# A Fourier neural operator's mixing weights centred on GpSimd instead of VectorE

## The chip, the cores and the metric

One core of one Trainium2 chip runs the whole program. The metric is the device time of one execution in microseconds (us). The engines are TensorE (PE), VectorE (DVE), ScalarE (ACT), GpSimd (POOL) and SyncE (SP), which issues all transfers.

## What is computed

The input is 64 images of 64 x 64 pixels. A Fourier neural operator comes first, then a small transformer-like tower on the resulting 64 x 64 tokens per image. Cut to the part that matters:

```python
h = layer_norm(x @ fc0_w + fc0_b, ln0_g, ln0_b)
for i in range(LAYERS):                      # 4 layers, 32 channels
    x_ft = rfft2(h)
    out_ft[:, :, :M1, :M2] = einsum('bixy,ioxy->boxy', x_ft[:, :, :M1, :M2], w1)
    out_ft[:, :, -M1:, :M2] = einsum('bixy,ioxy->boxy', x_ft[:, :, -M1:, :M2], w2)
    h = irfft2(out_ft) + einsum('bchw,oc->bohw', h, conv_w[i]) + conv_b[i]
    h = layer_norm(h, ln_g[i], ln_b[i])      # over the channels
    if i < LAYERS - 1:
        h = gelu(h)
h = fc3(gelu(fc2(gelu(fc1(h)))))
...
```

w1 and w2 are complex, 32 x 32 channels times 12 x 12 modes each, and differ by layer.

## The kernel before

**Phases.** The program has five phases over the pixels with a mixing between each two: "first" (fc0, layer norm, forward transform), mixing of layer 0, "mid" three times (inverse transform, convolution, layer norm, gelu, forward transform), each followed by a mixing, and "last" with the pointwise network. The token part follows. A phase handles 16 groups of four images. The groups run in hardware loops: two groups written out, two loops of six groups, one loop of two, and the end written out.

**The order.** Each engine goes through a group by the table `ORDER`: a list of steps per engine and phase. A name is a step, the number behind the point is which of its parts, a minus sign behind it says that it belongs to the group before. The steps of PE are `xt` (input transposed) or `i1` (first half of the inverse transform, L1181), `acc` (second half, the convolution added, L1209 and L1217; in first the product with fc0, L1199), `turn` (normalised values transposed, L1235), `back` (transposed again, L1246), `f1` and `f2` (forward transform, L1260, L1274). ScalarE copies PSUM out (`acc`, L1371), squares (`sq`, L1381), applies gain, bias and gelu (`gelu`, L1392), copies rows (`back`, L1396) and stores the spectrum (`pack`, L1402). VectorE transposes 32 x 32 blocks out of PSUM (`i1`, L1512; `f1`, L1544; `f2`, L1550), sums squares (`red`, L1519), takes the inverse root by seven small instructions (`rs`, function `root`, L209 to L215) and scales (`scale`, L1533). `i1`, `f1` and `f2` share one PSUM bank pair, pD; `acc` uses pA alone, `turn` pT alone.

**The centring.** Layer norm subtracts the channels' mean, so the kernel takes it out of the weights instead: from every mixing weight the mean over the 32 output channels is subtracted. The weights of a layer lie in `w_sb` as two slots of 128 partitions x 32 x 144 values (slot 0 also has its sign turned on half of the partitions). Step `cen` of VectorE does it by slices of 24 modes: `cen.0` reduces over the channels (L1494), `cen.1` scales the sum to minus the mean (L1496), `cen.2` adds it to the weights (L1498). `inline` sets the slice by the loop's counter: six slices of slot 0 in the first loop of six groups and six of slot 1 in the second, 36 instructions per layer, whose number the semaphore `w_centred` counts. Outside these two loops `cen` is skipped. The mixing on PE waits for all 36 (L1140 are its matmuls). SyncE issues the weight loads (L972) in the phase ahead of the mixing: at its beginning in first, behind the first group's `y_in` loads in mid. GpSimd has nothing to do up to the last mixing; then it clears some memory and later splits the token part's weights into two halves of precision (L824, L826).

Of the kernel before, what the change touches and what calls it, by code (L numbers as in the profile page):

```python
# [51 lines left out]
def constants():  # L52
# [45 lines left out]
    for b in range(2):  # L98
        for q in range(M1 + 1):
            iy[:, b, q, b] = np.cos(ang(q, y))  # L100
        for q in range(1, M1 + 1):
# [41 lines left out]
    "w_loaded":      (0, 8 * 16, 0, 0),  # L143
    "w_centred":     (0, 36, 0, 0),
    "y_bias":        (0, 1, 0, 0),
# [6 lines left out]
    "first": {  # L152
        "PE": ("xt.0 turn.2- acc.0 back.2- turn.3- acc.1 back.3- acc.2 turn.0 f1.1- acc.3 f1.0- back.0 turn.1 f2.0- "
               "back.1 f2.1-"),
        "ACT": ("xt.0 gelu.2- acc.0 sq.0 back.2- gelu.3- acc.1 sq.1 back.3- acc.2 sq.2 gelu.0 acc.3 sq.3 back.0 "
                "gelu.1 back.1 pack.0- pack.1-"),
        "DVE": ("red.0 cen.0 rs.0 scale.0 red.1 rs.1 f1.1- scale.1 f1.0- red.2 red.3 f2.0- rs.2 f2.1- scale.2 rs.3 "
                "cen.1 scale.3 cen.2"),
    },
    "mid": {  # L160
        "PE": ("i1.0 turn.2- back.1- acc.0 i1.1 turn.3- back.2- acc.1 back.3- acc.2 f1.1- turn.0 f1.0- acc.3 f2.0- "
               "turn.1 f2.1- back.0"),
        "ACT": ("back.1- acc.0 sq.0 gelu.3- back.2- acc.1 sq.1 back.3- acc.2 sq.2 gelu.0 acc.3 sq.3 pack.0- gelu.1 "
                "back.0 pack.1- gelu.2"),
        "DVE": ("red.3- i1.0 rs.3- scale.3- cen.0 cen.1 i1.1 red.0 rs.0 scale.0 red.1 rs.1 f1.1- scale.1 red.2 f1.0- "
                "rs.2 f2.0- cen.2 scale.2 f2.1-"),
    },
# [50 lines left out]
def build(nc, ins, out_ap, B):  # L218
# [18 lines left out]
    with ctx:  # L237
# [48 lines left out]
        cbias, cb_sum, cv_sum = small[:, 352:384], small[:, 384:385], small[:, 388:392]  # L286
        w_mean = small[:, 400:424]

# [22 lines left out]
        def param(rows, cols):  # L311
# [48 lines left out]
                 "turned", "h_new_ok", "x_loaded", "y_loaded", "y_clear", "packed", "h_loaded0", "h_loaded1", "stored0", "stored1", "fc0_clear", "y_stored", "w_loaded",  # L360
                 "w_centred", "mix_a_full", "mix_a_free", "mix_b_full", "mix_b_free", "y_bias", "conv_cleared", "conv_loaded", "conv_chain", "cst_loaded", "ln_loaded",
                 "fc0_loaded", "fc0_chain", "mlp_cleared", "mlp_loaded", "normed", "eps_set"]
# [467 lines left out]
        def alone(eng):  # L830

            eng.sem_inc(s["passed"], 1)
# [269 lines left out]
        @block.gpsimd  # L1102
        def _(pool):
            L = LAYERS - 1
            pool.wait_ge(s["mix_a_full"], at("mix_a", "mix", L, 0, 12))
            pool.wait_ge(s["mix_b_full"], at("mix_b", "mix", L, 0, 12))
            pool.memset(w_sb[:, 0:1024], 0.0).then_inc(s["mlp_cleared"], 1)
            pool.wait_ge(s["mlp_cleared"], 1)
            pool.memset(spec[:, 0:at_col[0]], 0.0).then_inc(s["par_cleared"], 1)
            pool.wait_ge(s["par_cleared"], 1)  # L1110

            pool.memset(XT[64:128, :], 0.0).then_inc(s["ones_set"], 1)
            pool.wait_ge(s["ones_set"], 1)
            pool.memset(XT[64:65, :], 1.0).then_inc(s["ones_set"], 1)
            pool.wait_ge(s["ones_set"], 2)
            token_pool(pool)
# [3 lines left out]
        def _(pe):  # L1120
            pe.wait_ge(s["cst_loaded"], 16)

            def mix(L):
                pe.wait_ge(s["w_centred"], at("w_centred", "mix", L, 0, 36) + 1)
                alone(pe)
# [312 lines left out]
        def _(dve):  # L1438
            dve.memset(pD[:], 0.0).then_inc(s["d_free"], 1)
            dve.sem_inc(s["a_free"], 1)  # L1440
            dve.sem_inc(s["w_centred"], 1)
            for i in range(2):
# [15 lines left out]
            def mix(L):  # L1458
# [10 lines left out]
                for k in range(12):  # L1469
# [4 lines left out]
                    if k == 1:  # L1474
# [5 lines left out]
                                                 in1=dc, op0=ALU.mult, op1=ALU.add).then_inc(s["y_bias"], 1)  # L1480

            centring = {}

            def cen(n, g):

                L, i, part = centring["L"], centring["i"], centring["part"]
                w = w_v[:, part, :, bass.ds(24 * i, 24)]
                first = 18 * part + n
                if n == 0 and part == 0:
                    dve.wait_ge(s["w_loaded"], 128 * L + 128)  # L1490
                dve.wait_ge(s["w_centred"], at("w_centred", "mix", L, 0, first) + 1 + 3 * i)
                alone(dve)
                if n == 0:
                    ins_ = dve.reduce_sum(w_mean, w.rearrange("p o m -> p m o"), axis=AX)  # L1494
                elif n == 1:
                    ins_ = dve.tensor_scalar(w_mean, w_mean, const["sign"][:, 1:2] if part == 0 else -1.0 / C, None, ALU.mult)  # L1496
                else:
                    ins_ = dve.scalar_tensor_tensor(out=w, in0=w, scalar=const["sign"][:, 0:1] if part == 0 else 1.0,  # L1498
                                                    in1=w_mean.rearrange("p (o m) -> p o m", o=1).broadcast_to([P, C, 24]),
                                                    op0=ALU.mult, op1=ALU.add)  # L1500
                ins_.then_inc(s["w_centred"], 1)

            def steps(p):
# [48 lines left out]

                return dict(cen=cen, i1=i1, red=red, rs=rs, scale=scale, turn=turn, f1=f1, f2=f2)

# [5 lines left out]

            phases(dve, "DVE", mix, steps, before_last, centring)
            token_dve(dve)
# [30 lines left out]
```

## Time and profile before

| | |
|---|---|
| runs | 3419.32, 3420.4, 3575.1 us; median 3420.4 us |
| profiled execution, own time | 3420.23 us |
| span of its profile | 3418.5 us |
| instructions profiled | 77905 |
| mean granted clock of TensorE | 0.936 of full |

The span is the time from the first instruction that the profile shows to the end of the last. Below, "busy" is the time in which an engine executes, "idle before" the time the engine stood still ahead of an instruction, and the name behind "<-" what it waited for. L numbers are lines of the kernel. The sections of the page are: busy times by engine, the span in 40 slices, transfers, the chain that ended last, groups of instructions, and the transfers' issues.

### The profile page before, as it was taken

Reading aid. Unit: us, or ns where it says so; the run is one execution under the profiler, and the core shown is the slowest. Engines: PE = TensorE matmul, PEld = TensorE weight load, DVE = VectorE, ACT = ScalarE, POOL = GpSimd, SP = SyncE. Lnnn points to the kernel's source line nnn. Section 1 sums busy time; section 2 is a strip of 40 time slices with the busy share of each in tenths; the row PEclk is TensorE's granted clock in tenths of the full one; section 3 lists DMA queues with packets and bytes.
Section 4 is the critical chain, followed back from the end, with each engine's and each line's share of the span. In section 5 each row is a group of like instructions: output and inputs, shape, how many; then the busy total and the mean of one; then the engine's idle time right before and its main releaser. Section 6 shows DMA issues by size and latency. Waiting matters only on the chain.

```text
span 3418.5 us, 77905 instructions
## 1 busy us (share of the span) xinstructions
PE 2958.7 (87%) x29936; PEld 1877.1 (55%) x29936; DVE 2143.1 (63%) x3982; ACT 1960.9 (57%) x2300; POOL 28.0 (1%) x12
## 2 busy tenths in 40 slices
PE   6888859999859999859999859999999997983994
PEld 3445446666546666536666534444444446971894
DVE  5888738888638888638888724454444535236457
ACT  5777626666526666526666517777777762432451
POOL 0000000000000000000000010000000001000000
PEclk9999879999979999969999979999999997996897
DMA  4222364444464444464444444111111100000000
GB/s 118 93 96 93 109 163 159 165 165 161 150 156 159 158 168 163 144 151 172 158 158 165 137 106 92 46 56 53 56 44 44 53 1 1 1 1 0 1 1 13
DMA packets 114136, 335.43 MB, mean 98 GB/s; under 512 B 46040, under 2 KB 78040, under 8 KB 78168
## 3 DMA queue, kind: packets, MB, share of 16 engines
q1 hardware_dynamic: 114008, 333.50, 30.4%
q8 instruction: 107, 1.75, 0.2%
q14 instruction: 21, 0.17, 0.0%
HBM read 179.31 MB, written 154.14 MB: 98 GB/s over the span
## 4 chain that ended last, share of the span: by engine, by line
PE 72%; DVE 13%; issue 5%; ACT 4%; DMA 3%; SPq 1%; DVEq 0%; ACTq 0%
PE pA L1209 14%; PE pA L1217 7%; PE pT L1303 7%; PE pD L1260 4%; PE pT L1235 4%; PE pD L1292 4%; PE pD L1274 4%; PE pD L467 3%; PE pA L467 3%; PE pS L1246 3%; PE pD L1181 3%; DVE arena L1550 2%; DVE w_sb L1533 2%; DVE arena L1544 2%; PE pT L459 2%
## 5 line engine op out<-in xcount | busy, mean ns | idle before, releaser
L1519 DVE TENSOR_REDUCE small<-w_sb 128x32 f32<-128x1056 f32 x320 | 395.5, 1240 | 341.6 <-ACT w_sb L1381 339.0
L1209 PEld LDWEIGHTS pA<-conv_bd,h_in 128*128 128x128 f32 x4096 | 482.2, 193 | 121.4 <-issue 96.7
L1209 PE MATMUL pA<-conv_bd,h_in 128*128 128x128 f32 x4096 | 521.3, 281 | 15.3 <-ACT w_sb L1371 4.3
L1371 ACT COPY w_sb<-pA 128x1024 f32<-128x1024 f32 x256 | 259.5, 1014 | 443.1 <-PE pA L1217 408.0
L1533 DVE SCALAR_TENSOR_TENSOR w_sb<-w_sb,small 128x1024 f32<-128x1024 f32 x320 | 386.4, 1212 | 5.3
L1392 ACT ACTIVATE h_new<-pT,bet,gam 128x1024 f32<-128x1024 f32 x256 | 307.0, 1199 | 96.1 <-PE pT L1235 88.9
L1381 ACT ACTIVATE w_sb<-w_sb 128x1024 f32<-128x1024 f32 x320 | 339.1, 1060 | 14.7
L1235 PE MATMUL pT<-cst,w_sb 128*128 128x128 f32 x2048 | 282.8, 282 | 34.8 <-DVE w_sb L1533 32.9
L1235 PEld LDWEIGHTS pT<-cst,w_sb 128*128 128x128 f32 x2048 | 225.8, 143 | 153.4 <-issue 125.3
L1246 PEld LDWEIGHTS pS<-cst,h_new 128*128 128x128 f32 x2048 | 231.7, 144 | 135.5 <-issue 82.3
L1396 ACT COPY h_rows<-pS 128x1024 f32<-128x1024 f32 x256 | 256.9, 1003 | 85.3 <-PE pS L1246 84.1
L1246 PE MATMUL pS<-cst,h_new 128*128 128x128 f32 x2048 | 281.2, 282 | 21.7 <-ACT h_new L1392 17.7
L1217 PE MATMUL pA<-arena,cst 64*64 64x512 f32 x2048 | 279.4, 616 | 0.0
L1303 PE MATMUL pT<-w_sb 128*64 128x512 f32 x1024 | 269.4, 614 | 2.7 <-ACT w_sb L1416 1.5
L1274 PE MATMUL pD<-arena,cst 64*32 64x384 f32 (+1 forms) x4096 | 214.6, 510 | 22.0 <-DVE arena L1550 16.1
L1544 DVE STREAM_TRANSPOSE arena<-pD 128x1024 f32<-128x1024 f32 x128 | 159.5, 1246 | 53.9 <-PE pD L1260 49.3
L1512 DVE STREAM_TRANSPOSE arena<-pD 128x1024 f32<-128x1024 f32 x96 | 119.9, 1249 | 109.2 <-PE pD L1181 108.5
L1416 ACT ACTIVATE w_sb<-pT,w_sb 128x512 f32<-128x512 f32 x256 | 173.0, 685 | 12.2 <-PE pT L1303 10.8
L1413 ACT ACTIVATE w_sb<-pD,w_sb 128x1024 f32<-128x1024 f32 x128 | 142.4, 1113 | 60.9 <-PE pD L1292 37.1
L1550 DVE STREAM_TRANSPOSE arena<-pD 128x768 f32<-128x768 f32 x128 | 125.4, 980 | 80.7 <-PE pD L1274 80.7
L1260 PE MATMUL pD<-h_rows,cst 64*32 64x512 f32 x2048 | 146.3, 627 | 34.2 <-DVE arena L1544 26.1
L1181 PE MATMUL pD<-y_in,cst 48*32 48x192 f32 (+1 forms) x3072 | 92.2, 348 | 82.7 <-DMA y_in<-y_scratch 72.5
(298 smaller groups left out, 4062.8 us busy)
## 6 DMA issues: line engine op xcount, KB each, us to landing
h_scratch<-h_new SPq DMA_DIRECT2D x128, 1024.0 KB, 4.2
h_in<-h_scratch SPq DMA_DIRECT2D x128, 1024.0 KB, 5.0
y_scratch<-arena SPq DMA_DIRECT2D x16, 1152.0 KB, 10.0
y_in<-y_scratch SPq DMA_DIRECT2D x512, 36.0 KB
w_sb<-in_L_tok_w1r_dram SPq DMA_DIRECT2D x8, 576.0 KB, 9.2
w_sb<-in_L_tok_w1i_dram SPq DMA_DIRECT2D x8, 576.0 KB, 9.0
w_sb<-in_L_tok_w2r_dram SPq DMA_DIRECT2D x8, 576.0 KB, 18.9
w_sb<-in_L_tok_w2i_dram SPq DMA_DIRECT2D x8, 576.0 KB, 18.9
```

What stands on the lines that cost most here:

```text
L1209: pe.matmul(pA[:, c:c + 128], h_in[:, 1024 * n + c:1024 * n + c + 128], conv_bd[:], start=(j == 0), stop=False, skip_group_check=True)
L1217: mm = pe.matmul(pA[64 * b:64 * b + 64, 512 * t:512 * t + 512].rearrange("p (x o) -> p o x", o=C), const["idft_y"][rows, 64 * b:64 * b + 6 ...
L1235: mm = pe.transpose(bank[:, 128 * j:128 * j + 128], raw[n][:, 128 * j:128 * j + 128], ident)
L1246: mm = pe.transpose(bank[:, 128 * j:128 * j + 128], h_new[:, 1024 * n + 128 * j:1024 * n + 128 * j + 128], ident)
L1260: mm = pe.matmul(out[q:q + 32, b], const["dft_y"][rows, NQ * b:NQ * b + NQ], src[rows, t, 32 * xh:32 * xh + 32, 16 * ch:16 * ch + 16], sta ...
L1274: mm = pe.matmul(out.rearrange("p (q h c) -> p h c q", h=2, c=16), const["dft_x"][rows, 128 * part + 32 * j:128 * part + 32 * j + 32], TA[ ...
L1303: mm = pe.matmul(bank[64 * j:64 * j + 64, :], fc2_w, G1[m % 2][:, 512 * j:512 * j + 512], start=True, stop=True)
L1371: act.copy(raw[n], pA[:]).then_inc(s["copied"], 1)
L1381: act.activation(sq[n % 2][:, :, 0:C], raw[n].rearrange("p (x o) -> p x o", o=C), ACT.Square, scale=float(C) ** -0.5).then_inc(s["squared" ...
L1392: act.activation(h_new[:, 1024 * n:1024 * n + 1024], pT[:], ACT.Gelu if ph == "mid" else ACT.Identity, bias=bet[:, col], scale=gam[:, col] ...
L1519: dve.reduce_sum(var[n], sq[n % 2], axis=AX).then_inc(s["summed"], 1)
L1533: dve.scalar_tensor_tensor(out=z, in0=z, scalar=ROOT_SCALE, in1=r.broadcast_to([P, 32, C]), op0=ALU.mult, op1=ALU.mult).then_inc(s["normed ...
```

## The change

The centring leaves VectorE. GpSimd does it in one piece per layer as soon as the eight weight loads have landed, by blocks of 72 modes: (slot 0) the sign, then a tree of additions that folds 32 channels to 16, 8, 4, 2 and 1 in a scratch tile `tree` inside `w_sb`, a scaling by -1/32, and one addition to the weights. Each instruction waits for the one before. The semaphore `w_centred` now counts layers. The order tables of "first" and "mid" are written anew without `cen`.

```diff
-    "w_centred":     (0, 36, 0, 0),
+    "w_centred":     (0, 1, 0, 0),
...
     "first": {
...
-        "DVE": ("red.0 cen.0 rs.0 scale.0 red.1 rs.1 f1.1- scale.1 f1.0- red.2 red.3 f2.0- rs.2 f2.1- scale.2 rs.3 "
-                "cen.1 scale.3 cen.2"),
+        "DVE": ("scale.3- red.0 rs.0 scale.0 red.1 rs.1 f1.0- red.2 f1.1- scale.1 f2.0- rs.2 f2.1- scale.2 red.3 rs.3"),
     },
     "mid": {
...
-        "DVE": ("red.3- i1.0 rs.3- scale.3- cen.0 cen.1 i1.1 red.0 rs.0 scale.0 red.1 rs.1 f1.1- scale.1 red.2 f1.0- "
-                "rs.2 f2.0- cen.2 scale.2 f2.1-"),
+        "DVE": ("i1.0 rs.3- scale.3- i1.1 red.0 rs.0 scale.0 red.1 rs.1 f1.0- scale.1 red.2 f1.1- rs.2 f2.0- scale.2 "
+                "f2.1- red.3"),
...
-        w_mean = small[:, 400:424]
+        tree = w_sb[:, 16512:17664]
...
         @block.gpsimd
         def _(pool):
+            def centre_weights(L):
+
+                pool.wait_ge(s["w_loaded"], 128 * L + 128)
+                alone(pool)
+                pool.sem_clear(s["tree"])
+                k = 0
+
+                def after(ins_):
+                    nonlocal k
+                    k += 1
+                    ins_.then_inc(s["tree"], 1)
+                    pool.wait_ge(s["tree"], k)
+
+                for slot in range(2):
+                    for m in range(0, M1 * M2, 72):
+                        w = w_v[:, slot, :, m:m + 72]
+                        part = lambda n: tree[:, 0:72 * n].rearrange("p (o m) -> p o m", o=n)
+                        if slot == 0:
+                            after(pool.tensor_scalar(w, w, const["sign"][:, 0:1], None, ALU.mult))
+                        after(pool.tensor_tensor(part(16), w[:, 0:16], w[:, 16:32], ALU.add))
+                        for n in (8, 4, 2, 1):
+                            after(pool.tensor_tensor(part(n), part(2 * n)[:, 0:n], part(2 * n)[:, n:2 * n], ALU.add))
+                        after(pool.tensor_scalar(part(1), part(1), -1.0 / C, None, ALU.mult))
+                        after(pool.tensor_tensor(w, w, part(1).broadcast_to([P, C, 72]), ALU.add))
+                pool.sem_inc(s["w_centred"], 1)
+
+            centre_weights(0)
+            with pool.Fori(0, LAYERS - 1) as L:
+                centre_weights(L + 1)
...
             def mix(L):
-                pe.wait_ge(s["w_centred"], at("w_centred", "mix", L, 0, 36) + 1)
+                pe.wait_ge(s["w_centred"], at("w_centred", "mix", L, 0, 1))
...
-            phases(dve, "DVE", mix, steps, before_last, centring)
+            phases(dve, "DVE", mix, steps, before_last)
```

PE's and ACT's lists of the two phases change as follows: in first, `turn.2- acc.0 back.2- turn.3- acc.1` becomes `turn.2- acc.0 back.1- acc.1 back.2- turn.3-`, and `turn.1` moves between `f2.0-` and `f2.1-`; in mid, `f1.0-` and `f1.1-` change places. ACT's list follows PE's.

VectorE at the start of the first loop of mid, before (L1512 is `i1`, L215 the last of `root`, L1533 `scale`, L1494 and L1496 `cen.0` and `cen.1`):

```order
L215 SCALAR_TENSOR_TENSOR small<-small 128x32
L1533 SCALAR_TENSOR_TENSOR w_sb<-w_sb,small 128x1024
L1490 ISA
L1491 ISA
L1494 ISA
L1494 TENSOR_REDUCE small<-w_sb 128x24
L1491 ISA
L1496 TENSOR_SCALAR small<-small,cst 128x24
L868 REGISTER_ALU
L1512 STREAM_TRANSPOSE arena<-pD 128x1024
```

The same place in the changed kernel (L1518 is `i1`, L214 the last of `root`, L1539 `scale`, L1525 `red`):

```order
L214 SCALAR_TENSOR_TENSOR small<-small 128x32
L1539 SCALAR_TENSOR_TENSOR w_sb<-w_sb,small 128x1024
L867 REGISTER_ALU
L1518 STREAM_TRANSPOSE arena<-pD 128x1024
L1524 ISA
L1525 TENSOR_REDUCE small<-w_sb 128x32
```

Between `scale.3` and the transpose `i1.1` the reduction and its scaling are gone; the rest stands as it did.

GpSimd's first block of a layer in the changed kernel (before, there is nothing here):

```order
L1121 TENSOR_SCALAR w_sb<-w_sb,cst 128x32x72
L1122 TENSOR_TENSOR w_sb<-w_sb 128x1152
L1124 TENSOR_TENSOR w_sb<-w_sb 128x576
L1124 TENSOR_TENSOR w_sb<-w_sb 128x288
L1124 TENSOR_TENSOR w_sb<-w_sb 128x144
L1124 TENSOR_TENSOR w_sb<-w_sb 128x72
L1125 TENSOR_SCALAR w_sb<-w_sb 128x72
L1126 TENSOR_TENSOR w_sb<-w_sb 128x32x72
```

It has eight such instructions in each block of slot 0 and seven in each of slot 1, 30 per layer, one behind the other.

## Rows read from the trace of the kernel before

**Rows 1.** The page: busy time, share of the span and instructions of each engine.

```profile
PE 2958.7 (87%) x29936; PEld 1877.1 (55%) x29936; DVE 2143.1 (63%) x3982; ACT 1960.9 (57%) x2300; POOL 28.0 (1%) x12
```

**Rows 2.** Time line of ScalarE (start, duration, line, idle before): `pack` one group apart.

```profile
213.29 0.43 ACT L1402 COPY spec<-arena 128x288 f32 x1
237.56 0.43 ACT L1402 COPY spec<-arena 128x288 f32 x1
...
382.34 0.44 ACT L1402 COPY spec<-arena 128x288 f32 x1
405.73 0.43 ACT L1402 COPY spec<-arena 128x288 f32 x1
...
669.41 0.43 ACT L1402 COPY spec<-arena 128x288 f32 x1 [0.53 <-DVE arena L1550]
697.05 0.43 ACT L1402 COPY spec<-arena 128x288 f32 x1 [0.53 <-DVE arena L1550]
...
890.17 0.43 ACT L1402 COPY spec<-arena 128x288 f32 x1 [0.53 <-DVE arena L1550]
917.92 0.43 ACT L1402 COPY spec<-arena 128x288 f32 x1 [0.53 <-DVE arena L1550]
```

**Rows 3.** By stretch: length; PE, PEld, DVE, ACT, POOL busy; clock; DMA share, GB/s.

```profile
213.30:237.60 24.30, 21.28 (x199) 11.91 (x191) 21.18 (x44) 18.27 (x21) 0.00 (x0) 1.00 0.25 96
382.30:405.70 23.40, 20.98 (x195) 11.98 (x186) 18.81 (x41) 18.29 (x20) 0.00 (x0) 1.00 0.23 92
669.40:697.10 27.70, 26.62 (x324) 17.82 (x326) 23.88 (x46) 17.44 (x19) 0.00 (x0) 1.00 0.45 161
890.20:917.90 27.70, 26.80 (x320) 17.80 (x320) 21.37 (x43) 17.36 (x18) 0.00 (x0) 1.00 0.25 101
1018.40:1046.10 27.70, 26.46 (x280) 18.29 (x280) 18.21 (x40) 14.61 (x14) 0.00 (x0) 0.89 0.54 200
```

**Rows 4.** Time line of TensorE in a mid group: its two longest waits.

```profile
672.37 0.91 PE L1181 MATMUL pD<-y_in,cst 48*32 48x208 f32 x32 [0.27 <-DVE arena L1550]
...
690.25 1.09 PE L1260 MATMUL pD<-h_rows,cst 64*32 64x512 f32 x16 [0.48 <-DVE arena L1544]
```

**Rows 5.** Time line of TensorE in a group of first: its longest wait.

```profile
240.74 1.09 PE L1235 MATMUL pT<-cst,w_sb 128*128 128x128 f32 x8 [1.30 <-DVE w_sb L1533]
```

**Rows 6.** Groups of VectorE's instructions (count, busy us, mean ns, idle before).

```profile
L1533 DVE SCALAR_TENSOR_TENSOR w_sb<-w_sb,small 128x1024 f32<-128x1024 f32 x320 | 386.4, 1212 | 5.3
...
L1494 DVE TENSOR_REDUCE small<-w_sb 128x24 f32 x48 | 70.9, 1477 | 0.0
...
L1498 DVE SCALAR_TENSOR_TENSOR w_sb<-w_sb,cst,small 128x768 f32 x24 | 23.6, 985 | 0.0
L1498 DVE SCALAR_TENSOR_TENSOR w_sb<-w_sb,small 128x768 f32 x24 | 22.2, 925 | 0.0
```

**Rows 7.** Time line of GpSimd and VectorE in the token part.

```profile
2860.44 1.89 POOL L824 CAST w1a_hi<-spec 128x2048 fp32r<-128x2048 f32 x1 [844.54 <-DVEq L671]
2862.41 4.55 POOL L826 TENSOR_TENSOR w1a_lo<-spec,w1a_hi 128x2048 fp32r<-128x2048 f32 x1
2862.97 0.69 DVE L679 TENSOR_TENSOR XT_split<-pS,XT_split 64x512 fp32r<-64x512 f32 x1 [2.75 <-ACT XT_split L564]
```

**Rows 8.** Weight loads: the page's time to landing, the last issues in first and mid.

```profile
w_sb<-in_L_tok_w2r_dram SPq DMA_DIRECT2D x8, 576.0 KB, 18.9
...
22.48 0.42 SPq L972 DMA_DIRECT2D w_sb<-in_L_tok_w2r_dram  x1
...
994.63 0.37 SPq L972 DMA_DIRECT2D w_sb<-in_L_tok_w2r_dram  x1
```

**Rows 9.** Time line of VectorE: `root` and `scale` in mid's second group.

```profile
1021.87 0.14 DVE L209 TENSOR_SCALAR small<-small 128x32 int32<-128x32 int32 x1
1022.05 0.19 DVE L210 TENSOR_TENSOR small<-small 128x32 f32<-128x32 f32 x1
1022.27 0.19 DVE L211 TENSOR_TENSOR small<-small 128x32 f32<-128x32 f32 x1
...
1023.40 1.22 DVE L1533 SCALAR_TENSOR_TENSOR w_sb<-w_sb,small 128x1024 f32<-128x1024 f32 x1
```

More of the change, by code:

```diff
@@ L152 @@
     "first": {
[L153 to L156, printed above, removed]
-        "DVE": ("red.0 cen.0 rs.0 scale.0 red.1 rs.1 f1.1- scale.1 f1.0- red.2 red.3 f2.0- rs.2 f2.1- scale.2 rs.3 "
-                "cen.1 scale.3 cen.2"),
+        "PE": ("xt.0 turn.2- acc.0 back.1- acc.1 back.2- turn.3- acc.2 back.3- turn.0 f1.0- acc.3 f1.1- back.0 f2.0- "
+               "turn.1 f2.1-"),
+        "ACT": ("xt.0 gelu.2- acc.0 back.1- sq.0 acc.1 back.2- gelu.3- sq.1 back.3- acc.2 sq.2 gelu.0 acc.3 back.0 "
+                "sq.3 gelu.1 pack.0- pack.1-"),
+        "DVE": ("scale.3- red.0 rs.0 scale.0 red.1 rs.1 f1.0- red.2 f1.1- scale.1 f2.0- rs.2 f2.1- scale.2 red.3 rs.3"),
     },
     "mid": {
-        "PE": ("i1.0 turn.2- back.1- acc.0 i1.1 turn.3- back.2- acc.1 back.3- acc.2 f1.1- turn.0 f1.0- acc.3 f2.0- "
+        "PE": ("i1.0 turn.2- back.1- acc.0 i1.1 turn.3- back.2- acc.1 back.3- acc.2 f1.0- turn.0 f1.1- acc.3 f2.0- "
                "turn.1 f2.1- back.0"),
@@ L360, in build @@
                  "turned", "h_new_ok", "x_loaded", "y_loaded", "y_clear", "packed", "h_loaded0", "h_loaded1", "stored0", "stored1", "fc0_clear", "y_stored", "w_loaded",
-                 "w_centred", "mix_a_full", "mix_a_free", "mix_b_full", "mix_b_free", "y_bias", "conv_cleared", "conv_loaded", "conv_chain", "cst_loaded", "ln_loaded",
+                 "w_centred", "tree", "mix_a_full", "mix_a_free", "mix_b_full", "mix_b_free", "y_bias", "conv_cleared", "conv_loaded", "conv_chain", "cst_loaded", "ln_loaded",
                  "fc0_loaded", "fc0_chain", "mlp_cleared", "mlp_loaded", "normed", "eps_set"]
@@ L1440, in _ @@
             dve.sem_inc(s["a_free"], 1)
-            dve.sem_inc(s["w_centred"], 1)
             for i in range(2):
@@ L1480, in mix @@
                                                  in1=dc, op0=ALU.mult, op1=ALU.add).then_inc(s["y_bias"], 1)
[L1482 to L1501, printed above, removed]
             def steps(p):
@@ L1551, in f2 @@
                                   bank.rearrange("p (t n) -> p t n", t=2)[:, :, 0:384]).then_inc(s["d_free"], 1)
-                return dict(cen=cen, i1=i1, red=red, rs=rs, scale=scale, turn=turn, f1=f1, f2=f2)
+                return dict(i1=i1, red=red, rs=rs, scale=scale, turn=turn, f1=f1, f2=f2)
             def before_last():
```

## The prediction

> **What bounds the kernel now.** I read the page first, then the time line at one repeating event, then the busy time by stretch, and last the rows around single waits.
>
> The page shows TensorE busy 87% of the span, VectorE 63%, GpSimd 1% [rows 1]. Profiled execution 3420.23 us, span 3418.5 us, so 1.7 us lie around it; the median of the three runs is 3420.4 us, the same for this purpose.
>
> The repeating event is ScalarE's copy of a group's spectrum (`pack`, L1402), which gives the length of one group of the loop. Twelve of the 16 groups of each of the first four phases carry the centring, the last two do not, so the kernel itself shows what a group costs with and without it. In the phase "first" a group takes 237.56 - 213.29 = 24.3 us with it and 405.73 - 382.34 = 23.4 us without it [rows 2]. In "mid" it takes 697.05 - 669.41 = 27.6 us with it and 917.92 - 890.17 = 27.75 us without it [rows 2]. By stretch, TensorE is busy 26.6 of 27.7 us in a mid group, with the centring or without; VectorE falls from 23.9 to 21.4 us and nobody gains [rows 3]; TensorE's clock is the full one in both. TensorE's longest waits in such a group are 0.27 and 0.48 us, each for a transpose by which VectorE frees the one PSUM bank pD [rows 4]. So mid (three layers) is bound by TensorE. In first TensorE is busy 21.3 of 24.3 us [rows 3] and waits 1.30 us at one place for VectorE's `scale` [rows 5]: a chain through the engines bounds it.
>
> **The change part by part.** *Removed from VectorE.* 48 reductions of 1477 ns and 48 full updates of 985 and 925 ns: 70.9 + 23.6 + 22.2 = 116.7 us of busy time [rows 6], and 48 small scalings of 128 x 24 values, which at the 0.19 us of other small ones [rows 9] are 9 us more: 126 us, 2.6 us in each of 48 groups. In the 36 mid groups this lay beside TensorE: worth 0. There the new order is the old without `cen` (`red.3` only moves over the end of the loop, `f1.0` and `f1.1` change places), so TensorE's waits stay; both ends: 0 and all that TensorE is not busy, 45 x (27.7 - 26.8) = -40 us.
>
> *First phase.* The twelve groups fall at least to what the kernel shows without `cen`, if the new order is as good as the old: 12 x (24.3 - 23.4) = -11 us. The new order puts `back.1` behind `acc.0`, which fills one hole, but keeps `turn.2` right behind `xt.0` and `scale.2` behind the second `f2` transpose, where the 1.30 us arise. Ends: 0 (the order is no better than 24.3) and TensorE's busy time, 12 x (24.3 - 21.3) + 3 x (23.4 - 21.3) = -42 us. I take -11, the measured one.
>
> *Added on GpSimd.* Per layer four blocks (two slots, two halves of 72 columns). The only arithmetic rows of GpSimd are 4547 ns for 2048 elements with two inputs, 2.2 ns each, and 1889 ns with one, 0.92 ns each [rows 7]. A block has additions of 1152, 576, 288, 144, 72 and 2304 elements, 4536 x 2.2 = 10.0 us, and a scaling of 72; the two blocks of slot 0 have a multiplication of 2304 more, 2.1 us. 4 x 10.1 + 2 x 2.1 = 44.6 us; 30 instructions with 0.1 us of fixed time and the 0.08 us between two GpSimd instructions [rows 7] add about 5: 50 us per layer. The mixing needs the result only after 16 groups (some 440 us), so GpSimd's own length costs nothing; even at three times it would be hidden.
>
> *What lies beside it.* It starts when the eight weight loads have landed: issued by 994.63 us, 18.9 us to landing, so at about 1014 us in the second layer, and, issued by 22.9 us, at about 42 us in the first phase [rows 8]. It then covers nearly two groups. The first of them, 1018.4 to 1046.1 us, has TensorE busy 26.5 of 27.7 us already [rows 3], so what delays VectorE's `root` and `scale` there delays the end. A group has four `root` chains, six of whose instructions have two inputs in SBUF (0.19 us, 0.03 us apart), and four `scale`s with two (1.22 us) [rows 6, 9]: 28 such instructions.
>
> *What that costs* no row shows: VectorE's addition beside GpSimd's (0.69 us, as its 15 sisters) has one input in PSUM [rows 7]. Below it is 0. Above, VectorE is held whenever GpSimd runs, less what passes meanwhile: 50 us, less 8 before the first `root` of the group at 1021.87 us [rows 9], less 15 us that pass meanwhile, 27 us per layer, 4 x 27 = +108 us. (Of the group's 27.7 us VectorE is busy 18.2 [rows 3]; the 28 instructions are 24 x 0.19 + 4 x 1.22 = 9.5 of them, so 8.7 us of other work and 9.5 us idle are left, and I let 15 of these 18 pass under GpSimd.) I take a middle value: a run of VectorE instructions waits once, for the rest of the GpSimd instruction that it meets. The rest of an instruction met at random is the sum of squares over twice the sum: (4 x 5.1^2 + 4 x 2.6^2 + 2 x 2.2^2 + 4 x 1.3^2 + 4 x 0.7^2) / (2 x 50) = 1.5 us. Eight runs in a group (four chains, four `scale`s), 1.8 groups: 14 meetings, 21 us; a third falls where VectorE would have been idle: 14 us per layer, 4 x 14 = +56 us.
>
> The Trainium skill speaks against this change here. "SBUF — State Buffer", section "Who interferes with whom", says that a VectorE instruction with two SBUF inputs takes its second one through a read interface shared with GpSimd, and that the later one of two such instructions waits until the earlier has ended; one with a single SBUF input is not held. The 0.69 us beside GpSimd's addition agree with the second half [rows 7]; the first half no row of this kernel shows. By the rule the first rival below or the forecast would come true, and without it the second rival.
>
> *The rest.* Phase "last" and the token part (from about 2000 us) keep their instructions; the wait of the mixing for `w_centred` was met long before and is.
>
> Sum: 3420 - 11 + 0 + 56 = 3465 us.
>
> **Rivals.** (1) *VectorE and GpSimd take strict turns.* Each of the 28 two-input instructions in a group waits for a whole GpSimd instruction, because GpSimd's next one is ready while VectorE's 0.19 us run and VectorE's next comes 0.03 us after. A `root` chain then lasts six or seven GpSimd instructions instead of 1.53 us [rows 9], and `turn`, behind its `scale`, stands in TensorE's queue with everything after it. +108 us: 3420 - 11 + 108 = 3517 us, slower by 2.8%. It decides from 20 us per layer on (4 x 20 - 11 = 69 us). For it: four GpSimd instructions of 5 us and a TensorE with 1 us of slack a group. Against it: nothing in the trace shows any holding up.
> (2) *Nothing is held up.* The engines pass each other as in rows 7; only the first phase shows: 3420 - 11 = 3409 us. For it: those rows. Against it: they have one SBUF input.
> (3) *The new order closes TensorE's holes too.* Half of the 42 us in first, half of the 40 in mid, nothing held: 3420 - 21 - 20 = 3379 us. Against it: the mid order is the old one.
>
> **How the numbers follow.** Chances: forecast 0.38, rival 1 0.25, rival 2 0.32, rival 3 0.05. Range: below, 3395 us leaves out rival 3 and little of rival 2 (3409 less half its uncertain 28 us); above, 3525 us is rival 1 with a little over it, leaving out its tail. The likeliest case alone has 3435 to 3500. A measurement here tells about 2%, 68 us: slower than 3488 us are nine tenths of rival 1 and a fifth of the forecast, 0.22 + 0.08 = 0.30; faster than 3352 us needs more than rival 3: 0.02; within, 0.68.
>
> **What would show it.** In the profile after: the pack copies of first 23.4 us apart from the fourth group on, those of mid 27.6. VectorE's busy time down by about 126 us where the instructions keep their lengths; if the time held up is counted in them, L1539 (the `scale`) and the `root` lines have a mean above 1212 and 190 ns with single ones of 3 to 6 us, else idle time stands before them. GpSimd busy 4 x 50 us, the four stretches beginning near 42 us and some 30 us before the second pack copy of each mid phase. The groups under those stretches are longer by about 14 us in all by the forecast, 27 by rival 1, 0 by rival 2. The prediction is wrong if the groups without GpSimd differ from 23.4 and 27.6 us by over 0.5 us, if GpSimd runs for most of a phase (its per-element time then not 2.2 ns), or if TensorE waits for GpSimd before the mixing.

## The result and the profile after

The changed kernel takes 3516.91 us (3506.52, 3516.29, 3517.53, 3519.74), the kernel before beside it 3419.86 us: ratio 1.028, interval 1.0253 to 1.0306. It is slower by 97 us. The profiled execution is the shortest of the four (3506.52 us, span 3504.7 us), 86.2 us over the span before; the other 11 us of the median stand in no trace.

The page's row of busy times, which answers to [rows 1]:

```profile
PE 2978.5 (85%) x29936; PEld 1895.8 (54%) x29936; DVE 2159.9 (62%) x3838; ACT 1958.5 (56%) x2300; POOL 276.2 (8%) x132
```

VectorE has lost 144 instructions that took 126 us together, and yet it is busy 16.8 us longer. GpSimd has 248 us more. Where the time went is seen in the copies of `pack` (now L1430), one group apart, as in [rows 2] (each row is the first copy of its group); the first three rows are the first groups of "first", the last three those of the second "mid":

```profile
85.83 0.42 ACT L1430 COPY spec<-arena 128x288 f32<-128x288 f32 x1
...
121.40 0.42 ACT L1430 COPY spec<-arena 128x288 f32 x1
...
145.23 0.42 ACT L1430 COPY spec<-arena 128x288 f32 x1
...
1107.77 0.43 ACT L1430 COPY spec<-arena 128x288 f32<-128x288 f32 x1 [3.85 <-DVE arena L1556]
...
1141.95 0.43 ACT L1430 COPY spec<-arena 128x288 f32 x1 [0.54 <-DVE arena L1556]
...
1169.49 0.43 ACT L1430 COPY spec<-arena 128x288 f32 x1 [0.54 <-DVE arena L1556]
```

In first the first copy comes at 85.8 us, 18.4 us later than before, and the next group takes 35.6 us; those that follow take 23.8 us. In the second mid phase the first copy comes 121.4 us behind that of the last group of the phase ahead, before 103.0 us: again 18.4 us more. The interval behind it is 34.2 us (33.0 and 32.9 us in the other two mid phases), the others are 27.5 us, as good as before. The copy of the last group of the third mid phase comes at 2059.5 us, before at 1973.0 us: 86.5 us, the whole difference of the spans. So everything is lost in the first two groups of each phase, and nothing in the other fourteen. The same by stretch, with the columns of [rows 3]:

```profile
85.80:121.40 35.60, 23.92 (x204) 13.49 (x189) 32.99 (x44) 18.23 (x20) 21.32 (x13) 0.90 0.17 65
121.40:145.20 23.80, 21.22 (x196) 12.16 (x184) 18.94 (x40) 18.06 (x20) 0.00 (x0) 1.00 0.26 96
...
1107.80:1142.00 34.20, 29.40 (x325) 20.56 (x326) 29.73 (x43) 17.62 (x19) 18.33 (x8) 0.90 0.33 114
1142.00:1169.50 27.50, 26.57 (x320) 17.72 (x321) 21.38 (x43) 17.35 (x19) 0.00 (x0) 1.00 0.46 163
```

The same 43 instructions of VectorE take 29.73 us in the group under which GpSimd runs and 21.38 us in the next. In the 35.6 us of first VectorE is busy 93% of the time, TensorE 67%: there VectorE is the bound. TensorE's granted clock is 0.90 in both first rows and 1.00 in the groups behind them; TensorE stood still more often there, behind the `scale`s that came late. In the same group of mid the kernel before has 1.00. For about the same number of matmuls TensorE is busy 29.40 us in the first mid row and 26.57 us in the next.

The groups of instructions of VectorE name the victims (lines are shifted: `scale` is L1539, `root` L208 to L214):

```profile
L1539 DVE SCALAR_TENSOR_TENSOR w_sb<-w_sb,small 128x1024 f32<-128x1024 f32 x320 | 401.9, 1260 | 8.6 <-DVE small L214 3.3
...
L210 DVE TENSOR_TENSOR small<-small 128x32 f32<-128x32 f32 x320 | 104.5, 327 | 10.9
L208 DVE TENSOR_SCALAR small<-small 128x32 int32<-128x32 int32 x320 | 97.7, 305 | 53.9 <-DVE small L1525 35.6 <-DVE h_new L1545 18.0
...
L209 DVE TENSOR_TENSOR small<-small 128x32 f32<-128x32 f32 x320 | 61.5, 192 | 11.0
```

The mean is over 320 calls of which only 23 lie beside GpSimd, so a mean of 327 ns in place of 192 is 43 us in a few calls. The idle time before the instructions (last columns) has not grown: what an instruction is held is booked as its own duration. On TensorE a part of this time shows as waiting for `scale`, in the row of `turn` (L1263):

```profile
L1263 PE MATMUL pT<-cst,w_sb 128*128 128x128 f32 x2048 | 289.6, 286 | 78.3 <-DVE w_sb L1539 76.4
```

The same group of the kernel before (`turn` is L1235 there) waits 43.5 us less:

```profile
L1235 PE MATMUL pT<-cst,w_sb 128*128 128x128 f32 x2048 | 282.8, 282 | 34.8 <-DVE w_sb L1533 32.9 <-ACT h_new L1392 1.9
```

GpSimd's own groups, which the kernel before does not have:

```profile
L1126 POOL TENSOR_TENSOR w_sb<-w_sb 128x2304 f32<-128x2304 f32 x16 | 85.0, 5312 | 1.3
L1124 POOL TENSOR_TENSOR w_sb<-w_sb 128x576 f32<-128x576 f32 (+1 forms) x64 | 60.6, 947 | 5.0
L1121 POOL TENSOR_SCALAR w_sb<-w_sb,cst 128x2304 f32<-128x2304 f32 x8 | 49.1, 6133 | 1406.4 <-remote 1362.0
L1122 POOL TENSOR_TENSOR w_sb<-w_sb 128x1152 f32<-128x1152 f32 x16 | 46.0, 2876 | 1.3
```

Last, the time line of both engines in the second mid phase (start, duration), where one sees it happen:

```profile
1062.09 6.12 POOL L1121 TENSOR_SCALAR w_sb<-w_sb,cst 128x2304 f32<-128x2304 f32 x1 [472.60 <-remote]
...
1065.49 2.75 DVE L208 TENSOR_SCALAR small<-small 128x32 int32<-128x32 int32 x1
1068.27 0.19 DVE L209 TENSOR_TENSOR small<-small 128x32 f32<-128x32 f32 x1
1068.29 2.66 POOL L1122 TENSOR_TENSOR w_sb<-w_sb 128x1152 f32<-128x1152 f32 x1
1068.50 2.50 DVE L210 TENSOR_TENSOR small<-small 128x32 f32<-128x32 f32 x1
...
1076.17 1.20 DVE L1525 TENSOR_REDUCE small<-w_sb 128x32 f32<-128x1056 f32 x1
...
1081.01 6.15 POOL L1121 TENSOR_SCALAR w_sb<-w_sb,cst 128x2304 f32<-128x2304 f32 x1
1081.20 5.55 DVE L210 TENSOR_TENSOR small<-small 128x32 f32<-128x32 f32 x1
```

L210, 0.19 us of work, starts 0.19 us after GpSimd's multiplication by the sign and takes 5.55 us; 1081.20 + 5.55 = 1086.75, and GpSimd's next (L1122) starts at 1087.24. L208 of 1065.49 is held in the same way until 1068.24. L209 between them slips through in 0.19 us, and the reduction of 1076.17 runs its 1.20 us in the middle of GpSimd's next addition (1075.84 to 1080.91): it is not held.

### The profile page after: what moved, and what is told of

It is laid out like the page before. It is cut to its first block, busy times and chain, and to the rows that moved or that the text cites. A ratio compares the mean times of both kernels' runs of the same rounds, so it can differ in the third digit from the quotient of the medians.

```text
span 3504.7 us, 77607 instructions
## 1 busy us (share of the span) xinstructions
PE 2978.5 (85%) x29936; PEld 1895.8 (54%) x29936; DVE 2159.9 (62%) x3838; ACT 1958.5 (56%) x2300; POOL 276.2 (8%) x132
## 3 DMA queue, kind: packets, MB, share of 16 engines
q8 instruction: 107, 1.75, 0.2%
## 4 chain that ended last, share of the span: by engine, by line
PE 72%; DVE 15%; issue 4%; ACT 3%; DMA 3%; SPq 1%; DVEq 0%; ACTq 0%
PE pA L1237 13%; PE pT L1331 7%; PE pA L1245 7%; PE pD L1302 6%; PE pD L1288 4%; PE pD L1320 4%; PE pT L1263 3%; PE pD L466 3%; PE pA L466 3%; DVE arena L1556 3%; PE pS L1274 3%; PE pA L1227 3%; PE pD L1209 2%; DVE arena L1550 2%; PE pT L458 2%
## 5 line engine op out<-in xcount | busy, mean ns | idle before, releaser
L1525 DVE TENSOR_REDUCE small<-w_sb 128x32 f32<-128x1056 f32 x320 | 396.5, 1239 | 334.5 <-ACT w_sb L1409 330.2
L1237 PEld LDWEIGHTS pA<-conv_bd,h_in 128*128 128x128 f32 x4096 | 491.6, 196 | 123.8 <-issue 99.1
L1237 PE MATMUL pA<-conv_bd,h_in 128*128 128x128 f32 x4096 | 530.3, 284 | 15.3 <-ACT w_sb L1399 4.3
L1399 ACT COPY w_sb<-pA 128x1024 f32<-128x1024 f32 x256 | 259.6, 1014 | 452.9 <-PE pA L1245 428.8
L1539 DVE SCALAR_TENSOR_TENSOR w_sb<-w_sb,small 128x1024 f32<-128x1024 f32 x320 | 401.9, 1260 | 8.6 <-DVE small L214 3.3
L1263 PE MATMUL pT<-cst,w_sb 128*128 128x128 f32 x2048 | 289.6, 286 | 78.3 <-DVE w_sb L1539 76.4
L1263 PEld LDWEIGHTS pT<-cst,w_sb 128*128 128x128 f32 x2048 | 229.5, 145 | 198.4 <-issue 123.0
L1518 DVE STREAM_TRANSPOSE arena<-pD 128x1024 f32<-128x1024 f32 x96 | 119.9, 1249 | 153.8 <-PE pD L1209 152.9
L1121 POOL TENSOR_SCALAR w_sb<-w_sb,cst 128x2304 f32<-128x2304 f32 x8 | 49.1, 6133 | 1406.4 <-remote 1362.0
```

The lines of the kernel that those rows point to most:

```text
L1237: pe.matmul(pA[:, c:c + 128], h_in[:, 1024 * n + c:1024 * n + c + 128], conv_bd[:], start=(j == 0), stop=False, skip_group_check=True)
L1263: mm = pe.transpose(bank[:, 128 * j:128 * j + 128], raw[n][:, 128 * j:128 * j + 128], ident)
L1399: act.copy(raw[n], pA[:]).then_inc(s["copied"], 1)
L1525: dve.reduce_sum(var[n], sq[n % 2], axis=AX).then_inc(s["summed"], 1)
L1539: dve.scalar_tensor_tensor(out=z, in0=z, scalar=ROOT_SCALE, in1=r.broadcast_to([P, 32, C]), op0=ALU.mult, op1=ALU.mult).then_inc(s["normed ...
```

## The experiments

L208, which the text comes back to, is the first instruction of `root`: a `tensor_scalar` that multiplies and adds a constant on the bits taken as int32. It has one tensor as input; L209 to L214 and `scale` have two.

The theory after the result: the new orders cost or gain little, and GpSimd holds VectorE's instructions that read two operands from SBUF, each for the rest of GpSimd's instruction. The rival: the loss comes from the new orders, or from GpSimd's traffic as such.

In the table stands what each kernel loses up to the third mid phase's end (the first copy of its last group, here and below "the last copy") against a kernel with the same orders and no centring, with GpSimd's busy time per layer and the time that VectorE's `root` and `scale` lines took over their sum in that kernel.

| kernel | GpSimd per layer | held, four layers | lost, four layers |
|---|---|---|---|
| after | 62 us | 128 us | 102 us |
| e4, 36 writes of 1.75 us | 63 us | 34 us | 14 us |
| e5, 60 copies of 1.09 us | 67 us | 140 us | 123 us |
| e6, 14 additions of 3.7 us | 54 us | 141 us | 130 us |
| e7, 100 additions of 0.82 us | 84 us | 93 us | 61 us |
| e8, the centring paced | 68 us | 0 | 2 us |

e4 to e7 have the orders of after, e8 those of before without `cen`. In e5 to e7 one memset of 1.75 us stands ahead of the copies or additions and is counted. e1, e3 and e4 to e7 leave the weights uncentred; e2 and e8 centre them in full.

**The new orders alone.** The call of the centring does nothing, so the mixing weights go in as they are loaded.

```diff
                 pool.wait_ge(s["w_loaded"], 128 * L + 128)
...
-                for slot in range(2):
-                    for m in range(0, M1 * M2, 72):
-                        w = w_v[:, slot, :, m:m + 72]
...
-                        after(pool.tensor_tensor(w, w, part(1).broadcast_to([P, C, 72]), ALU.add))
```

> The changed kernel with the centring itself left out (GpSimd waits for the weights and raises the semaphore, nothing else), so the weights stay uncentred. Theory (GpSimd's instructions hold VectorE's, nothing else costs): the first phase keeps 23.8 us a group, mid 27.5, the groups under GpSimd's stretches fall back by 29 us in first and some 22 in each mid, in all about 97 us: 3410 us profiled, ratio 0.997. Rival (the new orders themselves cost time at the phases' starts): it stays above 3440 us.

Measured: 3408.11 us, ratio 0.9976 (0.9962 to 0.999). The last copy of first comes at 424.9 us (430.4 before), the last of the third mid phase at 1957.3 us (1973.0 before): 5.5 us gained in first and 10.2 in the three mid phases and the mixings between. All 16 groups of first are 23.8 to 24.1 us apart:

```profile
211.43 0.42 ACT L1419 COPY spec<-arena 128x288 f32 x1
...
235.26 0.42 ACT L1419 COPY spec<-arena 128x288 f32 x1
```

The orders do not cost the 97 us; the rest, 86.5 + 15.7 = 102.2 us, is GpSimd's. With GpSimd silent L208 takes 167 ns in the mean (305 in the changed kernel), L209 to L214 take 192 and `scale` 1208:

```profile
L208 DVE TENSOR_SCALAR small<-small 128x32 int32<-128x32 int32 x320 | 53.3, 167 | 53.9 <-DVE small L1514 35.6 <-DVE h_new L1534 18.0
```

How the loss reaches TensorE shows by the stretch up to the last copy of the third mid phase (columns as in [rows 3]), first the changed kernel, then e1:

```profile
0.00:2059.50 2059.50, 1731.12 (x20000) 1134.42 (x20000) 1487.48 (x2716) 1151.00 (x1210) 248.36 (x124) 0.93 0.43 140
0.00:1957.30 1957.30, 1703.13 (x20000) 1114.12 (x20000) 1361.36 (x2716) 1149.94 (x1209) 0.21 (x4) 0.95 0.45 148
```

For the same 20000 matmuls TensorE is busy 28 us longer, at a mean granted clock of 0.93 in place of 0.95; the other 74 us it stands still. So about a quarter of the loss is not waiting, but matmuls that ran slower while the waits broke them up.

**The old orders with GpSimd's centring.** `ORDER` is that of before, with `cen` taken out.

```diff
-        "DVE": ("scale.3- red.0 rs.0 scale.0 red.1 rs.1 f1.0- red.2 f1.1- scale.1 f2.0- rs.2 f2.1- scale.2 red.3 rs.3"),
+        "DVE": ("red.0 rs.0 scale.0 red.1 rs.1 f1.1- scale.1 f1.0- red.2 red.3 f2.0- rs.2 f2.1- scale.2 rs.3 "
+                " scale.3"),
```

> The changed kernel with the order lists of the kernel before, only without cen. Theory: GpSimd meets VectorE's instructions as in the changed kernel, 3500 to 3520 us; first runs at 23.4 us a group in place of 23.8, mid at 27.6 in place of 27.5, so within 5 us of the changed kernel. Rival (the new orders put VectorE's two-input instructions where GpSimd hurts): 3470 us or less.

Measured: 3510.18 us, ratio 1.0267 (1.0248 to 1.0286). The loss is there with the old orders too. The last copy of the third mid phase comes at 2064.1 us.

**The old orders without any centring** (both edits together; the centring is left out).

> The kernel before with cen taken out and nothing in its place (weights stay uncentred). Both theories: 12 x 0.9 = 11 us less in first, nothing in mid: 3409 us. If the centring on VectorE cost more than its own groups showed, less than 3400.

Measured: 3551.93 us, ratio 1.0395 (1.038 to 1.0411), the opposite of what a kernel with less work should give. The copies say that it has nothing to do with the phases over the pixels: groups of first are 23.4 us apart as the kernel before shows them without `cen`, first ends at 419.5 us and the third mid phase at 1954.0 us, 19.0 us earlier than before. Against e2, which is this kernel with GpSimd's centring, that is 110 us. The loss arises in the token part. Two views of the same stretch, first the kernel before:

```profile
3200.00:3300.00 100.00, 100.00 (x742) 93.88 (x740) 48.41 (x70) 50.72 (x75) 0.00 (x0) 1.00 0.00 1
3300.00:3400.00 100.00, 72.01 (x525) 65.78 (x524) 65.88 (x83) 32.12 (x47) 0.00 (x0) 0.88 0.00 1
```

and the kernel of this experiment:

```profile
3200.00:3300.00 100.00, 100.00 (x392) 92.47 (x392) 26.27 (x38) 26.79 (x39) 0.00 (x0) 0.50 0.00 1
3300.00:3400.00 100.00, 100.00 (x393) 92.47 (x393) 27.65 (x40) 26.79 (x39) 0.00 (x0) 0.50 0.00 0
3400.00:3500.00 100.00, 100.00 (x402) 93.16 (x401) 28.35 (x41) 23.36 (x34) 0.00 (x0) 0.50 0.00 0
```

TensorE is busy throughout and its clock stays at half (1.2 GHz) for 345 us, where the kernel before had it at half for 24 us before it rose to the full 2.4 GHz. All four runs of this kernel took 3549 to 3555 us, at a mean granted clock of 0.896 to 0.899 (0.936 in the kernel before). What keeps the clock down was not tried. The order of the phases is not it: e8 below has the same orders and reaches the end of the third mid phase 1.8 us later, and its token part runs at the usual clock. Of the kernel before one of the four runs beside the changed kernel took 3575.1 us, 155 us over the others, which is about this size; it has no profile, so whether it is the same is not known.

**Writes alone.** GpSimd does 36 memsets of 1984 values into an unused stretch of `w_sb` in place of the centring.

```diff
-                for slot in range(2):
...
+                pad = w_sb[:, 16448:18432]
+                after(pool.memset(pad, 0.0))
+                for _ in range(35):
+                    after(pool.memset(pad, 0.0))
```

> The centring replaced by 36 memsets of 128 x 1984 scratch values per layer, one waiting for the other, which read nothing: 36 x (1.7 + 0.08) = 63 us of GpSimd per layer, as long as the centring (uncentred weights). Theory A (what is shared is reading a second SBUF input): the root instructions L209 to L214 and the scale L1539 keep 0.19 and 1.22 us, the time is that of the kernel without centring, about 3410 us. Theory B (any GpSimd instruction holds them): root and scale are held as before, 3480 us or more. Between them: only L208, one input, is held, by 1 us or less each: 3415 to 3430 us.

Measured: 3421.39 us, ratio 1.0016 (1.0002 to 1.0031). Groups of VectorE:

```profile
L1532 DVE SCALAR_TENSOR_TENSOR w_sb<-w_sb,small 128x1024 f32<-128x1024 f32 x320 | 385.1, 1208 | 8.6 <-DVE small L214 3.3
L208 DVE TENSOR_SCALAR small<-small 128x32 int32<-128x32 int32 x320 | 87.0, 272 | 53.9 <-DVE small L1518 35.5 <-DVE h_new L1538 18.0
L209 DVE TENSOR_TENSOR small<-small 128x32 f32<-128x32 f32 x320 | 61.4, 192 | 11.0
```

Everything with two inputs keeps its length. Only L208, with its single input, is held (167 ns without GpSimd's work). GpSimd writing for 63 us per layer costs 3.6 us per layer. The time lies in the range written down for "only L208".

**One input read.** 60 copies of 992 values within that stretch, behind one memset (the edit against e4).

```diff
-                for _ in range(35):
-                    after(pool.memset(pad, 0.0))
+                for _ in range(60):
+                    after(pool.tensor_copy(pad[:, 0:992], pad[:, 992:1984]))
```

> The centring replaced by 60 copies of 128 x 992 scratch values per layer (one input, about 0.95 us each, 62 us in all; uncentred weights). Theory (what VectorE's second input shares is GpSimd's reading, however many inputs GpSimd has): root and scale are held as in the changed kernel, each hold 0.9 us at most; some 20 us per layer, 3490 us. Rival (only GpSimd's instructions with two inputs hold them): as with the memsets, 3421 us.

Measured: 3522.54 us, ratio 1.0303 (1.0286 to 1.032), 33 us above the 3490 expected by the theory and far from the rival. One operand read by GpSimd is enough. Time line of VectorE in the second mid phase:

```profile
1077.48 9.41 POOL L1119 COPY w_sb<-w_sb 128x992 f32<-128x992 f32 x8
1077.49 1.04 DVE L211 SCALAR_TENSOR_TENSOR small<-small 128x32 f32<-128x32 f32 x1
1078.57 1.04 DVE L212 SCALAR_TENSOR_TENSOR small<-small 128x32 f32<-128x32 f32 x1
1079.64 1.04 DVE L213 SCALAR_TENSOR_TENSOR small<-small 128x32 f32<-128x32 f32 x1
1080.72 1.04 DVE L214 SCALAR_TENSOR_TENSOR small<-small 128x32 f32<-128x32 f32 x1
```

Here the two engines take strict turns: each instruction of 0.19 us takes 1.04 us, one copy. All 139 two-input `root` instructions in GpSimd's four stretches are held.

**Long additions.** 14 additions of 1984 values (the edit against e4).

```diff
-                for _ in range(35):
-                    after(pool.memset(pad, 0.0))
+                for _ in range(14):
+                    after(pool.tensor_tensor(pad, pad, pad, ALU.add))
```

> 14 additions of 128 x 1984 scratch values per layer, 4.4 us each, 63 us in all (uncentred weights). Theory (VectorE and GpSimd share by turns, so the loss follows GpSimd's total time, whatever its instructions' length): 23 to 28 us per layer, 3500 to 3520 us. Rival (a run of VectorE's instructions waits once per meeting, so few long instructions cost less than many): under 3470 us.

Measured: 3548.12 us, ratio 1.0385 (1.0368 to 1.0403), the largest loss with the least work on GpSimd. Neither time written down came true (3500 to 3520 us if the loss followed GpSimd's total, under 3470 us if few long instructions cost less): the total does not set the loss. The same instructions in the time line:

```profile
1083.03 3.53 DVE L211 SCALAR_TENSOR_TENSOR small<-small 128x32 f32<-128x32 f32 x1
1086.59 0.19 DVE L212 SCALAR_TENSOR_TENSOR small<-small 128x32 f32<-128x32 f32 x1
1086.82 3.37 DVE L213 SCALAR_TENSOR_TENSOR small<-small 128x32 f32<-128x32 f32 x1
1090.22 0.19 DVE L214 SCALAR_TENSOR_TENSOR small<-small 128x32 f32<-128x32 f32 x1
1090.45 4.40 DVE L1532 SCALAR_TENSOR_TENSOR w_sb<-w_sb,small 128x1024 f32<-128x1024 f32 x1
1094.77 1.24 DVE L1511 STREAM_TRANSPOSE arena<-pD 128x1024 f32<-128x1024 f32 x1
```

Most instructions that are held wait for nearly a whole addition of 3.7 us, and the one behind passes; of the 68 two-input `root` instructions in the four stretches 34 are held. The transpose out of PSUM is not held.

**Short additions.** 100 additions of 248 values (the edit against e4): more instructions and more busy time, but short ones.

```diff
-                for _ in range(35):
-                    after(pool.memset(pad, 0.0))
+                for _ in range(100):
+                    after(pool.tensor_tensor(pad[:, 0:248], pad[:, 0:248], pad[:, 248:496], ALU.add))
```

> 100 additions of 128 x 248 scratch values per layer, some 0.65 us each and 0.08 us apart, 73 us in all (uncentred weights). Theory (turns): single holds are 0.65 us at most, but many, 20 to 30 us per layer, 3490 to 3530 us. Rival (short instructions let VectorE through): under 3460 us.

Measured: 3466.76 us, ratio 1.014 (1.0118 to 1.0161), between the two times written down. GpSimd is busy 84 us per layer, the most of all, and the loss is half of that of the long ones. So among additions the length of the one that VectorE meets counts for more than how long GpSimd works. Length is not all: the copies of e5 are hardly longer (1.09 us against 0.82) and lose twice as much. There every two-input instruction of `root` waits, here 167 of 265. The loss goes by how many are held times how long each waits; what decides who passes was not found.

**The centring paced.** The whole centring on GpSimd again, nothing left out, with the old orders (without `cen`). It is cut to twelve slices of 24 modes, one per group from the third group on, and GpSimd waits for VectorE's count of finished `scale`s (`normed`), so that it works where VectorE has only transposes out of PSUM and reductions ahead of it.

```diff
+                def scaled(g, n):
+                    pool.wait_ge(s["normed"], at("normed", ph, L, g, n + 1))
...
-                    for m in range(0, M1 * M2, 72):
-                        w = w_v[:, slot, :, m:m + 72]
+                    for i in range(6):
+                        b = i + 2 + 6 * slot
+                        w = w_v[:, slot, :, 24 * i:24 * i + 24]
...
+                        scaled(b - 1, 3)
```

> The real centring on GpSimd, with the order lists of the kernel before without cen, cut into slices of 24 modes, one slice per group in 12 groups, each part of it started by the semaphore of a scale behind which VectorE has 1.9 to 4.7 us of transposes, reductions or idle time. Theory (only meetings cost): the holds all but vanish, first 23.4 and mid 27.5 us a group, so 19 us earlier than the kernel before at the end of the last mid phase: 3400 us, if TensorE's clock in the token part behaves as in the kernel before; 3545 us if it stays at half there as in the run without centring in the old orders. Rival (GpSimd's work costs VectorE wherever it lies): 3450 us or more.

Measured: 3399.84 us (3395.42 to 3409.02) against 3418.01 us, ratio 0.9947 (0.993 to 0.9963): faster than the kernel before by 0.5%, a small gain but clear of 1, and as expected (3400 us). Time line of one slice in the second mid phase:

```profile
1039.93 2.21 POOL L1129 TENSOR_SCALAR w_sb<-w_sb,cst 128x768 f32<-128x768 f32 x1 [192.84 <-DVE w_sb L1559]
1041.34 1.25 DVE L1538 STREAM_TRANSPOSE arena<-pD 128x1024 f32<-128x1024 f32 x1 [1.63 <-PE pD L1229]
1042.22 1.00 POOL L1130 TENSOR_TENSOR w_sb<-w_sb 128x384 f32<-128x384 f32 x1
1042.70 1.25 DVE L1545 TENSOR_REDUCE small<-w_sb 128x32 f32<-128x1056 f32 x1
1043.30 0.59 POOL L1124 TENSOR_TENSOR w_sb<-w_sb 128x192 f32<-128x192 f32 x1
1044.18 0.18 DVE L209 TENSOR_SCALAR small<-small 128x32 int32<-128x32 int32 x1 [0.23 <-DVE small L1545]
```

GpSimd's three instructions lie under an idle stretch of VectorE, a transpose and a reduction, both 1.25 us as ever, and end 0.29 us before `root` begins. Over the run `root`'s two-input lines have 192 ns, its first line (L209 here) 166 ns and `scale` 1208 ns, as if GpSimd stood still, though it is busy 274 us more than before. The groups of first are 23.4 us apart, and the third mid phase ends at 1955.8 us, 17.2 us earlier than before: what removing the centring from VectorE is worth here, once nothing is held. The slices are smaller and placed at once; what each of the two is worth alone was not tried.

## Why the prediction was wrong

**"First phase, -11".** Right in kind. With the old order it would have held (e3: 23.4 us a group, 10.9 us by the end of first). The new order is worse than the old by 0.4 us a group, 23.8 us, so e1 shows 5.5 us. I had named that end and not taken it.

**"Mid, 0".** Nearly right: 27.5 us a group in place of 27.6, which is 8.0 us over three phases, and 2.2 us less between the phases; 10.2 us together in e1, within the range given (0 to -40 us).

**"GpSimd 50 us per layer".** Measured 62 us, 64 to 65 us from the first start to the last end. The long additions have the length that I took (5.07 us for 2304 elements, 2.2 ns each, in three of the four per layer; the other takes 6.0 us). The multiplication by the sign has one input like the cast of [rows 7], from which I took 0.92 ns an element; it takes 6.12 us, 2.66 ns, which is 8 of the 12 us. The 0.1 us of fixed time stood in no row; the additions of e8 (234 ns for 24 elements, 1819 ns for 768) give about 0.18 us. That its length costs nothing in itself held.

**"A run of VectorE instructions waits once: 14 us per layer, +56."** This is the step that failed. Its mechanism is the right one: an instruction of VectorE waits for the rest of one of GpSimd's, and TensorE waits behind it. Its size is not: 102 us, 25.5 per layer, against 56. Counting single instructions in the trace with over 0.1 us added gives, per layer, 16 to 21 held in place of 14, for 1.7 us each in place of 1.5, which makes 32 us held per layer in place of 21.
- What was left out is L208, since it has only one input. All 23 that lie under GpSimd are longer than usual (0.28 to 5.03 us), and they take 44 of the 128 us (305 ns in the mean of all, in place of 167), 11 us per layer: the whole excess of 32 over 21. e4 shows that L208 is held even by pure writes.
- The two-input instructions alone were held 84 us, 21 per layer, as forecast, but by other parts. A `root` chain does not wait once; it meets GpSimd again two or three instructions on: L208, L210, then L212 or L214. 47 two-input instructions of `root` were held, and only 7 of the 19 `scale`s, for each of which I had counted a wait.
- I let a third of the meetings fall where VectorE would have been idle. Of 128 us held 102 reach the end, a fifth less. In these 102 are the 28 us by which the same matmuls took longer at a lower clock, for which the sum had no term.

By this count 14 us become 25.5: about 7 from L208 and 4 from the share that was let off. It is bookkeeping, since each wait shifts what comes behind it.

**The first rival, strict turns, 3517 us.** The time came out as it gives, 3516.91 us, with 102 us where it has 108. Its picture is true for e5, where all of `root` waits for a copy each. In the changed kernel 47 of the 114 two-input `root` instructions beside GpSimd wait, but longer stretches of GpSimd and L208 make up for it. So its sum came true by two errors that cancel as much as by its mechanism. It had 25% and the forecast 38%; the evidence on which I weighed them, VectorE's addition beside GpSimd's in [rows 7], concerned an operand in PSUM and told nothing of these lines. The second rival (nothing held, 3409 us) is what e1 shows with GpSimd silent, 3408 us.

**What the profile was to show.** The pack copies, the four stretches of GpSimd and the held time inside the instructions' lengths stand as foretold, with single instructions of up to 5.5 us; the places were right and the excess was not, 25.5 us in place of 14. GpSimd's stretches began at 44.45 us (42 forecast) and 46 us before the first pack copy of a mid phase. The forecast's "some 30 us before the second pack copy" was misread: 1014 us lies 32 us before the first copy of the second mid phase in the kernel before (1046.14 us), and that copy now comes some 18 us later.

The Trainium skill's "SBUF — State Buffer", section "Who interferes with whom", says that the engines hold a shared pair of interfaces exclusively for whole instructions, that a VectorE instruction with two SBUF inputs is kept out only by a GpSimd instruction that reads, and that `tensor_scalar`, with its single input, can run in a two-port mode, which contends with GpSimd. The runs agree: L209 to L214 are held by reads (e5) and not by writes (e4), L208 by both; that L208 runs in such a mode no row here shows. The prediction told the section's sentence on one input without its condition, "outside the 2-port perf modes", and passed over the one on `tensor_scalar`; that is how L208 fell out of the count.

## What to carry to other kernels

In these runs work on GpSimd was free only where VectorE had nothing that reads two operands from SBUF, nor a small one-input `tensor_scalar` from SBUF to SBUF like L208; its reductions and its transposes out of PSUM were not held. Count every such instruction in a dependent chain, not the chain as one. Additions on GpSimd cost half as much when they were short (0.82 us against 3.7), but short copies of 1.09 us did not help. Letting GpSimd wait for a semaphore of VectorE's, so that it ran beside transposes, reductions and idle time, helped most: with smaller slices it turned a loss of 2.8% into a gain of 0.5%.

## What the runs showed of the hardware

- A held VectorE instruction shows no idle time before it. It shows as a long instruction: 5.55 us for 128x32 values beside 0.19 us. A mean over 320 calls hides it (327 ns).
- A one-input `tensor_scalar` of 128x32 int32 from SBUF to SBUF (L208) is held by GpSimd's memsets (272 ns in the mean, 1.72 us once), while two-input instructions are not.
- How the turns fall depends on GpSimd's instruction: with copies of 1.09 us every two-input `root` instruction waits (139 of 139, 1.04 us each), with additions of 3.7 us half of them (34 of 68), with additions of 0.82 us 167 of 265. Why they differ was not found.
- GpSimd's multiplication by a value per partition takes 2.66 ns an element, longer than its addition of two operands (2.2 ns) and nearly three times its cast (0.92 ns).
- Holding VectorE slowed TensorE's matmuls too: 1731.1 us busy in place of 1703.1 us for the same 20000, at a mean granted clock of 0.93 in place of 0.95.
- TensorE's clock stayed at half for 345 us of unbroken matmuls in e3, in all of whose runs the time was up by about 150 us. Its cause is open.
